# Two chained cross-attention layers on one core: an in-place product with five buffers, first loads and constants inside the first phase, inverses stored once, and new engine orders

## The chip, the cores and the metric

One Trainium2 chip, one of its cores. The time is that of one execution on the device in microseconds (us); the kernel before has a median of 2640.99 us over 3 runs (2639.41 to 2641.47). Engines: PE (TensorE), PEld (its weight loads), DVE (VectorE), ACT (ScalarE), POOL (GpSimd), SP (SyncE, which here issues every DMA).

## The reference

Two cross-attention layers in a row on x (64 batches x 256 tokens x 320 channels), 20 heads of 16, with a context of 77 tokens x 512:

```python
# layer 0
q, k, v = heads(x @ Wq.T), heads(ctx @ Wk.T), heads(ctx @ Wv.T)      # all 77 tokens
x = softmax(q k^T / 4) v @ Wo.T + bo + x
# layer 1: text = ctx[:73], ip = ctx[73:]
q = heads(x @ W_q);  probs_t = softmax(q k_t^T / 4)                  # 73 tokens
text_out = probs_t v_t
qsem = l2norm(probs_t @ text)                                       # per head, 512 wide
sem  = qsem @ l2norm(ip)^T                                          # 4 columns
probs_ip = softmax(q k_ip^T / 4 + 0.5 * sem) * mask                 # 4 columns
out = (text_out + probs_ip v_ip) @ W_out + b_out + x
```

## The kernel before

**First phase** (`keys_and_values`). PE makes keys, values, the Gram matrix of the context tokens and the image-token keys for all batches, in 8 chunks of 8 batches, as sums of three float16 products; ACT and DVE take the results out of PSUM, SP stores them in DRAM (`k_dram`, `v_dram`, `g_dram`, `c_dram`, `kip_dram`). The 616 value rows of a chunk and layer are stored when all five blocks of rows are ready, in two DMAs (L366, L368). A block of the program ends only when all its engines are through, SP's waits for the last stores included.

**Second phase** (`attention`). It begins with clears of tiles (L1161 on DVE, L1281 on POOL), loads of constants (L795) and of the image-token keys (L797, L799). Every engine waits at `all_ready` until all of it is done. Then comes a software pipeline over the 64 batches. In iteration i an engine goes through its string in `ORDER`; a word such as `1u0/3` is step `u`, number 0, of layer 1, for batch i - 3. Every engine works strictly in the order of its string, SP with its DMAs too.

Steps of the PE: `q` query projection, `s` scores (for maxima), `m` transpose of the maxima, `t` turned scores (three products and the maxima subtracted by a product with `sel`), `a` attend (and the sums for the denominators), `o` output projection. Layer 1 only: `u` Gram matrix times halved exponentials, `n` sums of products (the squared norm of the semantic query), `i` image-token scores, `p` attend with the image tokens. Steps `s`, `t` and `a` come in three parts, of which the first two hold two units of four heads and the third one unit.

Other engines: ACT takes q (`q`), maxima (`m`), exponentials (`t0` to `t4`), sums (`a`), makes halves (`h0` to `h4`, tile `eh`), residual plus bias (`r`), the float16 part of what was attended (`g`), norms (`n`), the exponential of the 4 columns (`f`). DVE makes the rest of q (`ql`), maxima (`s0` to `s4`), inverses (`d`), products `w0` to `w4`, the small softmax `y0` to `y20`, `p`, `o`. POOL makes `xh`, `xl` (the float16 parts of the input), `b0` to `b4` (e minus its half, tile `e2`), `at` (attended times inverses), `al`, `kb`, `vb`, `c`.

**The inverses' round trip.** A step `a` leaves denominators in a row of `ust`. SP moves them (`ds`, L837) to `den`; DVE inverts (`d`, L1191); SP stores the inverses in `r_dram` in two copies (`rw`, L861), moves numerators within `ust` (`sh`, four DMAs, L854), and loads the inverses spread over partitions (`rl`, L867) into `rb`. Then POOL `at` (L1297), ACT `g` (L1153), POOL `al` (L1302), PE `o`.

**The product for the norm.** For unit k POOL writes `e2[k % 3]`, DVE writes `wr[k % 3] = psum * e2[k % 3]` (L1198), PE sums `wr` over tokens with `pick` (L1037).

**PSUM.** Eight banks. `USES` lists for each bank the uses in the order of an iteration. A PE step waits until the use before it on each of its banks has been read: a `t` bank by the exponential of its number, an `s` bank by the maxima, an `a` bank by ACT's `a`, a `u` bank by DVE's `w`.

Of the kernel before, what the change touches and what calls it, by code (L numbers as in the profile page):

```python
# [1 line left out]

# [9 lines left out]
ALU = mybir.AluOpType  # L12
# [40 lines left out]
LOW_RING = 3  # L53
# [39 lines left out]
class Batch:  # L93
# [23 lines left out]
    def reached(self, eng, sem, each, k):  # L117
# [21 lines left out]
        1ns/4 1nl/4 1sh/4 1sl/4 1rw/4 1k/2 1st/5 1rl/4 1d/3 1ps/4 1c/2 0x/0 1v/2 1vi/4 1ds/3 1pl/4 0ds/1
        0v/0 0rw/1 0k/0 1ss/3 1g/2 0sh/1 0rl/1""",  # L140
# [82 lines left out]
def keys_and_values(nc, psum, ctx, ctxip, wk, wv, wq, wo, wk_ip, wv_ip, pmask_d, k_dram, v_dram, g_dram, c_dram,  # L223
                    kip_dram, vip_dram, wqs, wos, wqt, wot, rnorm):
# [4 lines left out]
    with ExitStack() as stack:  # L229
# [12 lines left out]
        rawp = [sb(f"raw_projection{n}", [P, CW, WC]) for n in (0, 1)]  # L242
# [41 lines left out]
        s_istored, s_gstored, s_vstored = sem("ip_keys_stored"), sem("gram_stored"), sem("values_stored")  # L284
# [3 lines left out]
        KSTORES, VSTORES = 6, 4  # L288
# [18 lines left out]
        def _(sp):  # L307
# [22 lines left out]
            def store(b, slot):  # L330
# [48 lines left out]
            for n in (0, 1):  # L379
                load_projection(n)  # L380
# [1073 lines left out]
```

## Time and profile before

| | |
|---|---|
| median of 3 runs | 2640.99 us |
| profiled execution, whole | 2627.46 us |
| its span, first to last instruction | 2625.7 us |
| busy share of PE, PEld | 89%, 55% |
| busy share of DVE, ACT, POOL | 66%, 66%, 60% |
| DMA queue q1, share of 16 engines | 41.6% |
| last product of the first phase / first of the second | 333 us / 359.54 us |

A busy share is an average over the first phase (up to 333 us), the filling of the pipeline, about 56 equal iterations and the draining from about 2490 us on. The chain of waits is followed back from the last instruction; a row of it is a stretch of time with what it was spent on. "issue" is time in which the engine waited for nothing that the profile shows; SPq is SP's sequencer issuing a DMA.

### The profile page before, as it was taken

The numbers are of one execution on the slowest core, as the hardware profiler recorded it, in microseconds if no ns is written. First come the engines' busy times: TensorE is split into PE (matmuls) and PEld (weight loads), VectorE is DVE, ScalarE is ACT, GpSimd is POOL, SyncE is SP. The second block draws the span as 40 slices with busy tenths as digits, with TensorE's granted clock in tenths as the row PEclk, the third lists the DMA queues.
The fourth block names the chain that finished last, engine by engine and source line by source line (L and its number), as shares of the span: only waits on it lengthen the run. The fifth ranks groups of instructions, "written<-read, shape, count | busy, mean of one in ns | idle before, by whom it ended". The sixth has DMA issues, their size and how long they took to land.

```text
span 2625.7 us, 90322 instructions
## 1 busy us (share of the span) xinstructions
PE 2329.1 (89%) x35896; PEld 1455.7 (55%) x35896; DVE 1724.0 (66%) x3053; ACT 1728.2 (66%) x2602; POOL 1580.1 (60%) x1055
## 2 busy tenths in 40 slices
PE   7899937989989999998999899999999999899984
PEld 5677724555555555555555555555555555555542
DVE  5533323777777777777777777777777777677764
ACT  3332315777777777777777777777777777777762
POOL 3121024666677666666666667777676666676663
PEclk9999968999999999999999999999999999999996
DMA  8667622343434433334334344334444343434331
GB/s 274 201 211 224 195 82 58 100 110 108 110 102 110 111 106 105 110 108 112 104 109 110 107 109 111 108 107 111 110 112 111 98 112 106 110 106 111 105 90 53
DMA packets 337021, 310.90 MB, mean 118 GB/s; under 512 B 179440, under 2 KB 280048, under 8 KB 336624
## 3 DMA queue, kind: packets, MB, share of 16 engines
q1 hardware_dynamic: 336624, 305.35, 41.6%
q8 instruction: 280, 4.59, 0.7%
q14 instruction: 117, 0.96, 0.1%
HBM read 164.66 MB, written 105.98 MB: 103 GB/s over the span
## 4 chain that ended last, share of the span: by engine, by line
PE 32%; DMA 15%; SPq 14%; ACT 10%; POOL 8%; issue 5%; DVE 3%; ACTq 0%; POOLq 0%; DVEq 0%
PE psum L927 12%; DMA rb<-r_dram 8%; DMA den<-ust 6%; SPq L854 6%; PE psum L1010 5%; ACT ef L1115 5%; PE psum L991 4%; POOL ust L1297 4%; PE psum L1024 4%; POOL al L1302 4%; SPq L861 3%; ACT ah L1153 2%; PE psum L930 2%; SPq L881 1%; ACT ust L1123 1%
## 5 line engine op out<-in xcount | busy, mean ns | idle before, releaser
L1115 ACT ACTIVATE ef<-psum 73x1024 f32<-73x1024 f32 (+1 forms) x640 | 636.9, 1015 | 266.1 <-PE psum L994 248.1
L1335 POOL TENSOR_TENSOR e<-ef,eh 73x1024 f32<-73x1024 f32 x320 | 681.9, 2131 | 81.5 <-ACT eh L1130 81.4
L1176 DVE TENSOR_REDUCE mneg<-psum 128x8 f16<-128x584 f32 (+1 forms) x640 | 464.2, 775 | 105.9 <-PE psum L959 91.5
L1198 DVE TENSOR_TENSOR wr<-psum,e 73x1024 f32<-73x1024 f32 x320 | 390.3, 1220 | 163.6 <-PE psum L1024 160.6
L991 PE MATMUL psum<-q_high,keys 32*73 32x256 f16 (+2 forms) x6144 | 323.8, 258 | 63.1 <-ACT ust L1123 32.0
L1010 PE MATMUL psum<-ef,values 128*32 128x256 f32 x5120 | 357.9, 388 | 4.4 <-DVE wr L1198 4.0
L1024 PE MATMUL psum<-eh,gram 128*73 128x512 f16 x1280 | 338.5, 387 | 12.9 <-ACT ef L1115 11.3
L1297 POOL TENSOR_TENSOR ust<-ust,rb 128x768 f32<-128x768 f32 x128 | 231.7, 1810 | 186.4 <-DMA rb<-r_dram 185.9
L1130 ACT ACTIVATE eh<-ef 73x1024 f16<-73x1024 f32 x320 | 315.6, 1045 | 0.0
L1123 ACT ACTIVATE ust<-psum 128x512 f32<-128x512 f32 x384 | 229.2, 597 | 122.7 <-PE psum L1010 121.9
L991 PEld LDWEIGHTS psum<-q_high,keys 32*73 32x73 f16 (+1 forms) x6144 | 187.6, 110 | 158.4 <-ACT ust L1123 45.5
L1302 POOL TENSOR_TENSOR al<-ust,ah 128x768 f16<-128x768 f32 x128 | 210.4, 1644 | 82.8 <-ACT ah L1153 82.8
L1183 DVE SCALAR_TENSOR_TENSOR q_low<-psum,q_high 128x640 f16<-128x640 f32 x128 | 105.5, 824 | 219.1 <-ACT q_high L1099 219.1
L1327 POOL TENSOR_TENSOR vb<-vi,vmask 96x128 f32<-96x128 f32 x64 | 25.5, 398 | 370.1 <-DMA vi<-vip_dram 370.1
L927 PE MATMUL psum<-ah,wo 128*128 128x256 f16 x1280 | 197.0, 277 | 57.4 <-POOL al L1302 56.9
L1292 POOL TENSOR_TENSOR xl<-x,xh 128x768 f16<-128x768 f32 x128 | 210.4, 1643 | 9.6
L1024 PEld LDWEIGHTS psum<-eh,gram 128*73 128x73 f16 x1280 | 122.2, 114 | 151.9 <-ACT ef L1115 41.2
L994 PE MATMUL psum<-mt,sel 32*73 32x256 f16 (+3 forms) x3072 | 205.4, 251 | 0.8 <-issue 0.8
L991 PE MATMUL psum<-q_low,keys 32*73 32x256 f16 (+3 forms) x3072 | 204.8, 251 | 0.0
L1153 ACT ACTIVATE ah<-ust 128x768 f16<-128x768 f32 x128 | 107.9, 843 | 140.7 <-POOL ust L1297 119.1
L1037 PE MATMUL psum<-wr,pick 128*32 128x256 f32 x2560 | 197.9, 392 | 0.7 <-DVE wr L1198 0.7
L1010 PEld LDWEIGHTS psum<-ef,values 128*32 128x32 f32 x5120 | 128.6, 109 | 118.9 <-issue 41.9
(162 smaller groups left out, 4553.5 us busy)
## 6 DMA issues: line engine op xcount, KB each, us to landing
rb<-r_dram SPq DMA_DIRECT2D x128, 384.0 KB, 4.1
keys<-k_dram SPq DMA_DIRECT2D x128, 231.0 KB, 2.8
values<-v_dram SPq DMA_DIRECT2D x128, 192.5 KB
x<-in_x SPq DMA_DIRECT2D x64, 384.0 KB, 3.6
ust<-ust SPq DMA_DIRECT2D x512, 48.0 KB, 2.1
v_dram<-vst SPq DMA_DIRECT2D x16, 1280.0 KB
out<-outt SPq DMA_DIRECT2D x64, 320.0 KB, 3.2
k_dram<-kst SPq DMA_DIRECT2D x32, 616.0 KB, 4.0
```

Of the source, the lines that this page charges most:

```text
L927: mm = pe.matmul(o[:, c * S:(c + 1) * S], a, data[:, k, :], **at_ends)
L991: pe.matmul(o, keys(l, low, c)[rows, e, 0:n], q[rows, cols], start=(low == 0 and q is qh[l]), stop=False)
L1010: mm = pe.matmul(row(l, f"a{c}")[j * SLOT:(j + 1) * SLOT, r * S:(r + 1) * S], va[l][:, h, :], e, start=True, stop=True)
L1024: mm = pe.matmul(banks(l, f"u{k}", 2)[0:n, r, :], gm[:, half, :], e, start=(half == 0), stop=(half == 1))
L1115: act.activation(ef[l][0:m, unit_heads(n), :].rearrange("t h s -> t (h s)"), src, ACT.Exp, scale=SM).then_inc(s_exp[l], 1)
L1123: act.activation(ust[l][:, b.parity(), :, c, :], src, ACT.Copy).then_inc(s_u[l], 1)
L1130: act.activation(eh[0:m, unit_heads(k), :], ef[1][0:m, unit_heads(k), :], ACT.Copy, scale=0.5)\
L1176: dve.tensor_reduce(dst, o, AX_X, ALU.max, negate=True).then_inc(s_max[l], 1)
L1198: dve.tensor_tensor(wr[0:m, k % LOW_RING, :, :].rearrange("t (r h) s -> t r (h s)", r=2), banks(l, f"u{k}", 2)[0:m, :, :], e2[0:m, k % LOW ...
L1297: pool.tensor_tensor(at(l, b), at(l, b), rb[l][:], ALU.mult).then_inc(s_at[l], 1)
L1302: pool.tensor_tensor(al[l][:], at(l, b), ah[l][:], ALU.subtract).then_inc(s_al[l], 1)
L1335: pool.tensor_tensor(e2[0:m, k % LOW_RING, :, :], ef[1][0:m, unit_heads(k), :], eh[0:m, unit_heads(k), :], ALU.subtract).then_inc(s_e2, 1)
```

## The change

1. **Product in place, five buffers.** `wr` goes. `e2` has five units; DVE multiplies in place; POOL's `b` of a unit waits only for the PE's `n` of the batch before.
2. **Inverses stored once.** `r_dram` has one copy; `rw` is one DMA instead of two, `rl` reads each head's row for 16 partitions instead of 8 + 8.
3. **Beginning of the second phase.** Constants, the first batch's x and (before the last two stores) its layer-0 keys are loaded in the first phase, its `xh` and `xl` made there, `kip` cleared there. `all_ready` goes; single steps wait for the clears. `eh` is cleared by DVE (as the float32 pattern of 128x2560) instead of POOL. Clears that the first steps need (`small_clears`) come first on POOL.
4. **First phase.** Values are stored block by block, five DMAs per chunk and layer, each as its block is ready. `rawp` lies over the raw value weights. The second pair's context is loaded before the output and query projections.
5. **New orders** on all five engines, and new `USES`.

```diff
 ORDER = {
     "pe": """
-        1t1/3 1n3/4 1n4/4 0s0/1 1a0/3 0s1/1 1t2/3 1u0/3 0s2/1 1o/5 0m/1 1u1/3 0o/2 0t0/1 1a1/3 1u2/3 1a2/3
...
+        1t2/3 1a0/3 0s2/1 1o/5 0m/1 1u1/3 0o/2 0t0/1 1u2/3 1a1/3 0t1/1 1q/2 0t2/1 0a0/1 1s0/2 0a1/1 1s1/2
+        0a2/1 1a2/3 1i/2 1s2/2 1u3/3 1m/2 1u4/3 1t0/2 0q/0 1n0/3 1p/4 1n1/3 1n2/3 0s0/0 1n3/3 1n4/3 1t1/2
+        0s1/0 1u0/2""",
...
+        1t3/3 1t4/3 1a0/3 0g/2 1h2/3 0m/1 1h3/3 1r/3 1h4/3 0t0/1 0t1/1 1a1/3 0t2/1 1f/4 0t3/1 1q/2 0t4/1
+        0a0/1 0a1/1 0a2/1 1a2/3 1i/2 1m/2 0r/0 1t0/2 1h0/2 0q/0 1t1/2 1h1/2 1g/4 1n/3 1t2/2""",
...
-        0al/2 1b2/3 1kb/2 1b3/3 1xh/2 1xl/2 1at/4 1vb/4 0xh/0 1b4/3 0xl/0 1c/2 1b0/2 1al/4 1b1/2 0at/1""",
+        1b1/3 1al/5 0at/2 0al/2 1kb/2 1b2/3 1xh/2 1xl/2 1b3/3 1b4/3 0xh/0 0xl/0 1vb/4 1at/4 1c/2 1b0/2""",
...
 USES = [
...
+    "1u1/3 0t1/1 0t3/1 0t4/1 1s0/2 1s3/2 1u3/3 0q/0 0s1/0 0s2/0 1u0/2",
+    "1o/5 0t1/1 0t3/1 0t4/1 1s0/2 1s2/2 1s4/2 1m/2 1t1/2 0s0/0 1t2/2 1u0/2",
...
-                for l in both:
-                    results_of("v", l, 0)
-                    dst = v_dram[l][bass.DynSlice(token, full * P), :].rearrange("(k p) n -> p k n", p=P)
-                    sp.dma_start(dst, vst[l][:, 0:full, :, :].rearrange("p k h d -> p k (h d)")).then_inc(s_vstored, 16)
...
+                    for c, (k0, m) in enumerate(VT):
+                        wait_taken(sp, b, slot, KV_USES.index(("v", l, c, 0)))
+                        dst = v_dram[l][bass.DynSlice(token + k0, m), :]
+                        sp.dma_start(dst, vst[l][0:m, c, :, :].rearrange("p h d -> p (h d)")).then_inc(s_vstored[l], 16)
...
+            for t, d in constants:
+                sp.dma_start(t[:], d).then_inc(s_const, 16)
+            sp.dma_start(early.xin[:], x[0:1, :, :, :].rearrange("a c p s -> p (a c) s")).then_inc(early.s_x, 16)
...
+            sp.wait_ge(s_kstored[0], 16 * KSTORES * 2 * (PAIRS - 1))
+            sp.dma_start(early.ke[:], k_dram[0][0:1, :, :].rearrange("a p n -> (a p) n")).then_inc(early.s_ke, 16)
...
+            pool.wait_ge(early.s_x, 16)
+            pool.tensor_copy(early.xh[:], early.xin[:]).then_inc(early.s_xh, 1)
...
-        dve_clears, pool_clears = [ef[0], ef[1]], [va[0], va[1], eh, wr, kip, mneg[0], mneg[1], gm]
+        small_clears, dve_clears, pool_clears = [mneg[0], mneg[1], va[0], va[1], gm], [ef[0], ef[1], eh], [e2]
...
             def store_inverses(l, b, n):
                 b.reached(sp, s_rd[l], 1, 1)
-                for copy in (0, 1):
-                    dst = r_dram[l][b.parity()][:, copy, :].rearrange("h (q i) -> h q i", i=QS)
-                    sp.dma_start(dst, rd[l][:, b.parity(), :]).then_inc(s_rw[l], 16)
+                dst = r_dram[l][b.parity()].rearrange("h (q i) -> (h q) i", i=QS)
+                sp.dma_start(dst, rd[l][:, b.parity(), :]).then_inc(s_rw[l], 16)
 
             def spread_inverses(l, b, n):
                 b.reached(sp, s_at[l], 1, 0)
-                b.reached(sp, s_rw[l], 32, 32)
-                src = r_dram[l][b.parity()].rearrange("h k n -> (h k) n").unsqueeze(1).to_broadcast([2 * HC, D // 2, CW * S])
+                b.reached(sp, s_rw[l], 16, 16)
+                src = r_dram[l][b.parity()].unsqueeze(1).to_broadcast([HC, D, CW * S])
...
             def weighted(l, b, k):
-                b.reached(dve, f_n, UNITS, k + 1 - LOW_RING if k >= LOW_RING else (4, 5, 3)[k] - UNITS)
                 b.reached(dve, s_e2, UNITS, k + 1)
                 b.reached(dve, f_u, UNITS, k + 1)
                 m = TXT[1]
...
+                rest = e2[0:m, k, :, :].rearrange("t (r h) s -> t r (h s)", r=2)
+                dve.tensor_tensor(rest, banks(l, f"u{k}", 2)[0:m, :, :], rest, ALU.mult).then_inc(s_wr, 1)
```

SP, in the stretch from layer 0's denominators to the spread inverses (`den`, `r_dram`, `ust`, `rb` are those of the round trip above; the suffix of `r_dram` is the batch's parity). Before:

```order
L837 DMA den<-ust 96x1x64
L815 DMA values<-v_dram 77x640
L861 DMA r_dram_1<-rd 8x12x64 x2
L810 DMA keys<-k_dram 128x924
L881 DMA s_dram<-sipst 3x32x256
L820 DMA gram<-g_dram 77x146
L854 DMA ust<-ust 16x768 x4
L867 DMA rb<-r_dram_1 128x1x768
```

After:

```order
L821 DMA values<-v_dram 77x640
L845 DMA den<-ust 96x1x64
L904 DMA pt<-p_dram 96x1x256
L821 DMA values<-v_dram 77x640
L814 DMA keys<-k_dram 128x924
L828 DMA gram<-g_dram 77x146
L868 DMA r_dram_1<-rd 96x64
L845 DMA den<-ust 96x1x64
L874 DMA rb<-r_dram_1 128x1x768
L862 DMA ust<-ust 16x768 x4
```

Between the store of the inverses and their spreading stood keys, image scores, Gram and four moves of numerators; now one move of layer 1's denominators stands there, and the numerators follow the spreading. Layer 1's values (the first row) now come ahead of the denominators' move.

PE, around unit 0 of the Gram product (`eh,gram` 73x512). Rows of 128x2x77 are layer 0's scores `s0`, `s1`; 73x128 are parts of layer 1's `t2`; `ef,values` is `a0`. Before:

```order
L959 MATMUL psum<-keys,q_high 128x2x77 x8
L1010 MATMUL psum<-ef,values 32x256 x8
L959 MATMUL psum<-keys,q_high 128x2x77 x8
L991 MATMUL psum<-q_high,keys 73x128 x4
L991 MATMUL psum<-q_low,keys 73x128 x4
L991 MATMUL psum<-q_high,keys 73x128 x4
L994 MATMUL psum<-mt,sel 73x128 x4
L991 MATMUL psum<-q_high,keys 73x128 x4
L991 MATMUL psum<-q_low,keys 73x128 x4
L991 MATMUL psum<-q_high,keys 73x128 x4
L994 MATMUL psum<-mt,sel 73x128 x4
L1024 MATMUL psum<-eh,gram 73x512 x4
```

After:

```order
L999 MATMUL psum<-mt,sel 73x256 x4
L964 MATMUL psum<-keys,q_high 128x2x77 x8
L1032 MATMUL psum<-eh,gram 73x512 x4
L996 MATMUL psum<-q_high,keys 73x128 x4
L996 MATMUL psum<-q_low,keys 73x128 x4
L996 MATMUL psum<-q_high,keys 73x128 x4
L999 MATMUL psum<-mt,sel 73x128 x4
L996 MATMUL psum<-q_high,keys 73x128 x4
L996 MATMUL psum<-q_low,keys 73x128 x4
L996 MATMUL psum<-q_high,keys 73x128 x4
L999 MATMUL psum<-mt,sel 73x128 x4
L1016 MATMUL psum<-ef,values 32x256 x8
```

Between the end of `t1` (the first row) and `u0` there is now only `s1`; the attend part and `t2` that stood there come behind.

## Rows read from the trace of the kernel before

**Rows 1.** Windows, 600 to 2500: busy us (count) of PE, PEld, DVE, ACT, POOL; PEclk, DMA share.
```profile
600.00:2500.00 1900.00, 1747.52 (x28777) 1055.51 (x28767) 1370.17 (x2408) 1417.37 (x2072) 1310.51 (x896) 1.00 0.40 108
```

**Rows 2.** Timeline of SP (start, us, what): loads of x for batches 6, 62, 63.
```profile
547.77 1.70 SPq L804 DMA_DIRECT2D x<-in_x  x1
...
2450.03 0.40 SPq L804 DMA_DIRECT2D x<-in_x  x1
2484.15 0.40 SPq L804 DMA_DIRECT2D x<-in_x  x1
```

**Rows 3.** Waits of PE, 600 to 2500: us in total, times, longest.
```profile
PE psum L927 <- POOL al L1302: 41.6, 47, 2.4
PE psum L991 <- ACT ust L1123: 26.8, 55, 0.5
PE psum L959 <- issue: 14.0, 54, 0.3
PE psum L959 <- ACT ef L1115: 13.7, 61, 0.5
PE psum L952 <- ACT ef L1115: 11.0, 56, 0.2
PE psum L1024 <- ACT ef L1115: 10.2, 56, 0.2
```

**Rows 4.** Chain that ended last, 1504 to 1525: start, us, what.
```profile
1505.53 3.39 DMA den<-ust
...
1509.59 0.71 SPq L861
...
1514.79 1.21 SPq L854
...
1516.10 3.75 DMA rb<-r_dram
...
1519.98 1.82 POOL ust L1297
...
1521.90 0.85 ACT ah L1153
...
1522.89 1.65 POOL al L1302
```

**Rows 5.** Timelines of ACT, DVE and PE in one iteration: start, us, what.
```profile
1509.02 1.93 ACT L1115 ACTIVATE ef<-psum 73x1024 f32<-73x1024 f32 x2 [1.34 <-PE psum L994]
1516.20 2.91 DVE L1176 TENSOR_REDUCE mneg<-psum 128x8 f16<-128x616 f32 x4 [0.93 <-PE psum L959]
1518.46 1.06 PE L1024 MATMUL psum<-eh,gram 128*73 128x512 f16 x4
```

**Rows 6.** Timelines of SP, DVE, POOL and PE between the phases.
```profile
333.96 0.47 SPq L368 DMA_DIRECT2D v_dram<-vst  x1
340.22 0.38 SPq L795 DMA_DIRECT2D ident<-in_ident  x1
341.36 4.33 DVE L1161 MEMSET ef<- 128x5120 f32 x1 [7.86 <-issue]
341.36 4.37 POOL L1281 MEMSET eh<- 128x5120 f16 x1
346.70 4.33 DVE L1161 MEMSET ef<- 128x5120 f32 x1 [1.01 <-issue]
359.54 1.01 PE L927 MATMUL psum<-xh,wq 128*128 128x256 f16 x4 [26.57 <-POOL xl L1292]
366.37 3.62 DVE L1176 TENSOR_REDUCE mneg<-psum 128x8 f16<-128x616 f32 x5 [0.56 <-PE psum L959]
```

**Rows 7.** DMA issues, 600 to 2500: count, KB each, median us from issue to landing.
```profile
rb<-r_dram SPq DMA_DIRECT2D x112, 384.0 KB, 4.2
ust<-ust SPq DMA_DIRECT2D x448, 48.0 KB, 2.1
```

**Rows 8.** Timeline of PE in the drain.
```profile
2612.99 1.23 PE L1064 MATMUL psum<-pt,vb 32*128 32x256 f32 x6 [12.98 <-DMA pt<-p_dram]
```

More of the change, by code:

```diff
@@ L1 @@
 from contextlib import ExitStack
+from dataclasses import dataclass
 import numpy as np
@@ L241, in keys_and_values @@
             split[name] = sb(f"split_{name}", [P, 2, EC, columns], F16)
[L242 removed]
+        rawp = [raw[v][:].rearrange("p k n -> p (k n)")[:, 0:CW * WC].rearrange("p (k n) -> p k n", n=WC)
+                for v in ("v0", "v1")]
         order = ["k0", "k1", "kt", "ki", "v0", "v1"]
@@ L401, in _ @@
             sp.wait_ge(s_last, 96)
+            sp.wait_ge(s_const, 16 * len(constants))
+            sp.wait_ge(s_keyless, 1)
             for half in (0, 1):
@@ L405, in _ @@
             sp.wait_ge(s_gstored, 16 * 2 * 2 * PAIRS)
-            sp.wait_ge(s_vstored, 16 * VSTORES * 2 * PAIRS)
+            for l in both:
+                sp.wait_ge(s_vstored[l], 16 * VSTORES * 2 * PAIRS)
         @block.tensor
@@ L489, in half_keys, with wait_stored @@
             return ktail[:, half, :, low, e, :]
-        def wait_stored(eng, b, slot, kind, half):
+        def wait_stored(eng, b, slot, kind, half, l):
             if kind in ("k", "kt"):
@@ L518, in chunk @@
                         continue
-                    wait_stored(act, b, slot, kind, half)
+                    wait_stored(act, b, slot, kind, half, l)
                     b.reached(act, s_filled, 2 * KU, slot * KU + u + 1)
@@ L569, in chunk @@
                         continue
-                    wait_stored(dve, b, slot, kind, half)
+                    wait_stored(dve, b, slot, kind, half, l)
                     b.reached(dve, s_filled, 2 * KU, slot * KU + u + 1)
@@ L635, in _ @@
             pool.memset(one[:], 1.0).then_inc(s_one, 1)
+            pool.memset(early.kip[:], 0.0).then_inc(s_keyless, 1)
             for l in both:
@@ L690, in attention @@
         ql = [sb(f"q_low{l}", [P, PW], F16) for l in both]
-        ke = [sb(f"keys{l}", [P, 2 * CW * 2 * T], F16) for l in both]
+        ke = [early.ke, sb("keys1", [P, 2 * CW * 2 * T], F16)]
         va = [sb(f"values{l}", [P, H, SLOT]) for l in both]
@@ L807, in load_keys @@
             def load_keys(l, b, n):
+                if l == 0 and first(b):
+                    return
                 b.reached(sp, f_t[l], CW, 0)
@@ L812, in load_values @@
             def load_values(l, b, n):
+                if first(b):
+                    sp.wait_ge(s_small, SMALL)
                 b.reached(sp, f_a[l], CW, 0)
@@ L817, in load_gram @@
             def load_gram(l, b, n):
+                if first(b):
+                    sp.wait_ge(s_small, SMALL)
                 b.reached(sp, f_u, UNITS, 0)
@@ L1106, in exponentials @@
             def exponentials(l, b, n):
+                if first(b):
+                    act.wait_ge(s_zero, CLEARED)
                 b.reached(act, f_a[l], CW, n // 2 + 1 - CW)
@@ L1167, in maxima @@
                 m = TXT[l]
+                if first(b):
+                    dve.wait_ge(s_small, SMALL)
                 b.reached(dve, f_m[l], 1, 0)
@@ L1279, in _ @@
         def _(pool):
+            for t in small_clears:
+                pool.memset(t[:], 0.0).then_inc(s_small, 1)
             for t in pool_clears:
                 pool.memset(t[:], 0.0).then_inc(s_zero, 1)
-            all_ready(pool)
             def high_input(l, b, n):
+                if l == 0 and first(b):
+                    return
                 b.reached(pool, f_q[l], 1, 0)
@@ L1289, in low_input @@
             def low_input(l, b, n):
+                if l == 0 and first(b):
+                    return
                 b.reached(pool, f_q[l], 1, 0)
@@ L1339, in _ @@
                                    "at": text_attended, "al": low_attended, "c": sem_values, "kb": ip_keys, "vb": ip_values, "b": rests})
+@dataclass
+class Early:
+    ident16: object
+    sel: object
+    pick: object
+    kmask: object
+    vmask: object
+    mask: object
+    bias: list
+    kip: object
+    xin: object
+    xh: object
+    xl: object
+    ke: object
+    s_x: object
+    s_ke: object
+    s_xh: object
+    s_xl: object
 def attention_stack_kernel(nc, x, ctx, ctxip, mask, wq, wk, wv, wo, bias, wk_ip, wv_ip, ident16_d, sel_d, pick_d,
@@ L1354, in attention_stack_kernel @@
     vip_dram = dram("vip_dram", (CW, B * IP, P))
-    r_dram = [[dram(f"r_dram{l}_{n}", (HC, 2, CW * S)) for n in (0, 1)] for l in both]
+    r_dram = [[dram(f"r_dram{l}_{n}", (HC, CW * S)) for n in (0, 1)] for l in both]
     n_dram = dram("n_dram", (P, S))
```

129 lines of the change are left out of this document (60 added, 69 removed), and 14 rows, old and new, of the table USES.

## The prediction

> **What bounds the kernel.** I read the windows first, then the loads of x for the length of an iteration, then PE's waits and the chain. Between 600 and 2500 us PE is busy 1747.5 of 1900 us, 92%, at a granted clock of 1.00, while DVE, ACT and POOL are at 69 to 75% [rows 1]. The loads of x for batches 6 and 62 are 1902.3 us apart, 56 iterations of 33.97 us [rows 2]. So PE works 0.92 x 33.97 = 31.24 us in each and stands 2.73 us. None of its matmuls goes or comes, so 31.24 us is a floor and the new orders can win at most 2.73 us an iteration. PE's waits say what the 2.73 is: 41.6 us for POOL's `al`, 26.8 for ACT's `ust`, and four groups of 10 to 14 us of about 0.2 us each time [rows 3]; over 55.9 iterations that is 0.74, 0.48 and 0.88 us. Some 0.6 is spread over smaller groups. The chain shows why `al` is late: it is the round trip of layer 0's inverses, from 1505.53 to 1524.54 us, of which the two stores, the keys, the scores, the Gram load and four moves of numerators stand between 1509.59 and 1516.10 on SP [rows 4]. This loop closes over PE's order and sets the pace with PE itself.
>
> The rest of the time lies at the ends. The first phase's last store is issued at 333.96, the second phase begins at 340.22, and PE's first product comes at 359.54 [rows 6].
>
> **The iteration, part by part.** I laid the new strings out along PE's 31.24 us with the durations of before. The places that decide:
>
> *The round trip.* `rw` is one DMA, 0.71 us of issue less. Between it and `rl` stands one move. The store must land first. No row has its landing; a 48 KB move within the chip's memory takes 2.1 us, a 384 KB load 4.2 [rows 7]; I take 2.1 (24 KB, near the first) and keep 4.2. So `rl` starts 2.1 us after the inverses instead of 6.5, and the numerators, now behind it, land 3 x 0.6 + 0.6 + 2.1 = 4.5 us after `rl`'s start, against 4.2 for `rb`: they are what is late next. The trip from the denominators' move to `al`'s end is then 3.4 + 0.7 + 2.1 + 4.5 + 1.9 + 1.0 + 1.75 = 15.4 us instead of 19.0 [rows 4]. The move itself stands behind layer 1's values, which now wait for `a2` of layer 1 (0.5 us later). Going by the new strings, 19 us of the iteration lie between layer 0's `a2` and `o`. So the 0.74 us for `al` go. What takes its place on POOL is order: `b1` and layer 1's `al` stand ahead of `at`. `h1` is ready some 4.9 us before the iteration's end; `b1` (2.1), `al` (1.65), `at` (1.8), ACT's `g` and `al` (1.65) end 5 us into the next, and PE comes to `o` at 5.5 us: 0.5 us of slack.
>
> *Unit 0 of the Gram product.* It uses banks 1 and 2 of the new table, behind layer 0's `s2` and layer 1's `t2`. `t1` ends, then only `s1` (0.3 us) lies before `u0`. The exponential `t2` starts 0.1 us after the end of `t1` and takes 1.0 (two in 1.93) [rows 5]; DVE's maxima `s2` come 0.1 us after `s1` and take 0.75 (four in 2.91) [rows 5]. Both end about 1.2 us after `t1`, so PE stands 0.9 us. `u0` takes 1.06, and `t2`, which needs exponential 3, follows it without a wait. This 0.9 replaces the 0.48 us for ACT's `ust`.
>
> *Other places.* `s2` of layer 0 waits for exponential 4 (0.1 to 0.2, as before); `u2` for DVE's `o` (0.1 us, instead of 0.18); `s0` of layer 1 for exponential 4 of layer 0 (0.2, as before); `q` of layer 1 gets `xl` with 0.4 us to spare, and with one product fewer of POOL ahead of it. The product in place has the same operands and shape, 1.22 us: nothing. Five buffers free POOL and DVE of each other; DVE waits at `w` for PE's Gram product, not for buffers, so alone they bring nothing and only allow the new POOL string. Taking a store away frees SP 1.4 us an iteration, which is seen only in the trip above.
>
> The new wait is 0.9 + 0.8 for the short ones + 0.2 left of the scattered 0.6 (the part for late transfers I take as gone) = 1.9 us, an iteration 31.24 + 1.9 = 33.1 us. That is 0.85 less, over 58 iterations (56 and some of the filling): 49 us. The ends of this: all waits as before, 0; all gone but the short ones, 0.8 us in place of 2.73, 112 us.
>
> **The ends of the phases.** The last values' store is now a block of 104 rows after four that are already on their way. The old last stores took from 333.96 to 340.1; a transfer of 2.1 to 4.2 us instead gives 336.5 to 338.5, a gain of 3. In the second phase the first x, its parts, the keys and constants are there, so PE starts at once. But DVE has its clears ahead of the maxima: two of 4.33 us with 1.1 and 1.0 us of pause, as before, and then `eh`. Its 2560 elements cost 2.2 us at the rate of the 5120 in 4.33 [rows 6]; at the full 4.4 of the POOL row it is 2.2 more. So DVE is free at 337 + 1.1 + 4.33 + 1.0 + 4.33 + 0.5 + 2.2 = 350.5, does `ql` (0.8) and begins the maxima at about 351.5 instead of 366.37. Gain up to here 14 us, the 3 included; bounds 10 and 18. PE's first projection is covered by the clears, whatever its clock. Each of the first two round trips, where PE does nothing else, is 2 us shorter (two stores are 1.4, numerators no longer ahead of `rl` 2.5, less the landing): 3 us. In the drain PE stands 13 us for the last small softmax [rows 8], a chain the change leaves as it is; some shorter round trips, 3 us.
>
> On the clear the Trainium skill has a rule (VectorE: DVE Perf Modes, Zero memsets can be issued as uint32): a memset costs one cycle per element whatever the type, and zeros may be written as 4-byte words. By it `eh` is 2560 elements here and the gain stays; the POOL row, 5120 elements of float16 in 4.37 us, agrees with the count by elements, and no row shows a halved one.
>
> In the first phase values' stores are 48 more, of 0.4 us of SP, which waits there for PE's results anyway; PE has no wait on a store in it. The constants add 9 issues before the first results' stores: no reader in the next 20 us. I take 0, bounds -3 and +3.
>
> Sum: 49 + 14 + 3 + 3 = 69 us off the profiled 2627.5: 2558. The median of the runs is 13.5 us above the profiled execution, so 2572 on its scale.
>
> **Rivals.**
> *Ends only.* PE's waits only change their names: the 0.9 us at `u0`, and 0.7 more at `o` because DMAs that land late meet POOL's string with 0.5 us of slack. For it: the gap at `al` varies up to 2.4 us [rows 3]. Against it: the trip is 3.6 us shorter. 2641 - 20 = 2621; with a part of the gain left, 2605 to 2628.
> *Nearly all waits go.* If `t2`'s exponential is earlier than I lay it (DVE and ACT ahead of PE), only the short waits stay: 2641 - 112 - 20 = 2509; half of that way 2535.
> *Slower: layer 1's tail holds layer 0's.* On POOL layer 1's `al` now stands ahead of layer 0's `at`; it needs ACT's `g`, that DVE's `p`, that PE's `p`, that the load of the probabilities, which on SP stands behind the values' wait and the denominators' move. If `al` is more than 0.5 us late, all of it goes into the iteration. The point where it decides is 0.5 + 0.85 + 20/58 = 1.7 us late. At 2.3 us late an iteration is 34.9, and the time 2641 - 20 + 58 x 0.93 = 2675. Against it: by my layout the load lands 3 us before PE's `p`.
> *It doesn't do what it says.* That starting PE earlier moves nothing, since DVE is held by clears: in my sum already; were the clears 8 us longer than laid, 8 us less.
>
> **Numbers.** Forecast 0.62 (own range 2545 to 2600), ends only 0.17, nearly all 0.14, slower 0.05, something within 0.2% of before 0.02. About 0.2%, 5 us, is what a measurement of this kernel tells from no change. Faster 0.93, same 0.02, slower 0.05. The range leaves out the slower case and the outer parts of the two neighbours: 2526 to 2617.
>
> **What would show it.** Right: loads of x 33.1 us apart; PE's wait for `al` gone from the top, a wait of the Gram product (`u0`) for ACT's exponential or DVE's maxima of about 0.9 us in every iteration as its largest; `rl` issued 2 to 2.5 us after the inverses; the first maxima near 351 us; the second phase at 337. Wrong: PE waiting for `al` as long as before (the order on POOL), a wait at `u0` under 0.4 or over 1.5 us, iterations under 32.5 or over 33.8 us, or a first phase that ends other than at 333 us.

## The result, and the profile after

The changed kernel takes 2718.17 us (median of 4 runs, 2710.15 to 2731.16) against 2640.2 of the kernel before beside it: 1.0304 times as long, 95% interval 1.0261 to 1.0347. It is slower, outside the predicted range of 2526 to 2617 us. The profiled execution has a span of 2708.4 us, 82.7 more than before.

Timeline of SP after (start, us, what): loads of x for batches 7 and 63. They answer to [rows 2].

```profile
576.65 0.41 SPq L806 DMA_DIRECT2D x<-in_x  x1
...
2566.55 0.41 SPq L806 DMA_DIRECT2D x<-in_x  x1
```

Before, the load for batch 7 was issued at 583.47 and the last at 2484.15. So the span's 82.7 us split without a rest: up to batch 7 the changed kernel is 6.8 us ahead; the 56 iterations take 1989.9 us instead of 1900.7, 35.53 each instead of 33.94, which is 89.2 more; the draining from the last x to the end takes 141.9 instead of 141.6.

The ends are as forecast. Timelines of SP, DVE, POOL and PE between the phases, after; they answer to [rows 6].

```profile
331.15 1.97 SPq L370 DMA_DIRECT2D v_dram<-vst  x2
336.23 0.65 SPq L797 DMA_DIRECT2D kip<-kip_dram  x1
336.41 0.72 PE L932 MATMUL psum<-xh,wq 128*128 128x256 f16 x4 [4.18 <-PEq L229]
337.36 4.33 DVE L1167 MEMSET ef<- 128x5120 f32 x1 [4.60 <-issue]
...
347.50 2.19 DVE L1167 MEMSET eh<- 128x2560 uint32 x1 [0.48 <-issue]
351.00 1.51 DVE L1183 TENSOR_REDUCE mneg<-psum 128x8 f16<-128x616 f32 x2 [0.63 <-PE psum L964]
```

The second phase starts at 336.2 instead of 340.2, the first maxima at 351.0 instead of 366.37. The loss lies in the iteration. Windows after, 600 to 2500, with the columns of [rows 1]:

```profile
600.00:2500.00 1900.00, 1670.05 (x27534) 1036.07 (x27536) 1306.33 (x2309) 1363.74 (x1983) 1256.32 (x855) 0.98 0.38 102
```

PE has 230 us without work in 1900 instead of 152, and the granted clock is 0.98 instead of 1.00. Waits of PE after, 600 to 2500 (us in total, times, longest), answering to [rows 3]:

```profile
PE psum L932 <- POOL xl L1301: 75.0, 35, 3.7
PE psum L1032 <- DVE mneg L1183: 52.7, 47, 1.4
PE psum L932 <- DVE e L1205: 42.9, 18, 3.1
...
PE psum L932 <- POOL al L1311: 8.2, 13, 1.1
```

The wait for `ust` is gone, the one for `al` nearly, and the forecast one at `u0` is there (second row, 1.1 us each). New are the first and the third. Both stand before layer 0's query projection; together 117.9 us in 53 iterations, 2.2 us each. The third row's releaser is DVE's product in place; I count it with the first, since both rows vanish together in the first experiment. POOL in turn waits for the load of x: waits of POOL, 600 to 2400.

```profile
POOL xh L1294 <- DMA x<-in_x: 330.2, 51, 7.8
```

Before, this wait was 1.0 us in the whole stretch. The chain of the changed kernel shows what makes x late (start, us, what):

```profile
1746.29 0.43 DVE psum L1244
1746.74 0.33 SPq L894
1747.18 0.59 SPq L862
...
1749.70 0.53 SPq L833
1750.33 0.66 SPq L874
1751.09 5.30 DMA x<-in_x
1756.51 0.83 POOL xh L1294
1757.48 1.65 POOL xl L1301
1759.27 1.91 PE psum L932 x16
```

L1244 is `y14` of layer 1, the addition of the visual sums (its tile goes by the name of psum); L894 is `sl`, SP's load of them; L862 numerators, L833 `c`, L874 `rb`, then x. SP stood before `sl` from 1740.91 on, the end of the issue before it. Waits of SP after, 600 to 2500 (L121 is a helper's line; its row here is SP waiting before `rl` for the stored inverses to land):

```profile
SPq L894 <- DVE psum L1244: 304.9, 54, 6.0
SPq L121 <- DMA r_dram<-rd: 156.7, 53, 3.8
```

The first row is 5.6 us in every iteration. The cause can be read in the strings: `sl` was `1sl/4` on SP, DVE's `y` steps are `1y14/4` in both kernels, and `sl` waits for `y14` of the batch before (`SIP_READ - STEPS`). At lag 4 that `y14` had run an iteration earlier. The new string has `1sl/3`, so the `y14` that it waits for is the one of the same iteration. `sip` has two halves, so `y14` two batches back would be enough. And x stands behind it, right behind the 384 KB of `rb`. DMA issues after, 600 to 2500 (count, KB, median us to landing), answering to [rows 7]:

```profile
rb<-r_dram SPq DMA_DIRECT2D x107, 384.0 KB
x<-in_x SPq DMA_DIRECT2D x54, 384.0 KB, 5.8
ust<-ust SPq DMA_DIRECT2D x428, 48.0 KB, 3.0
p_dram<-pip SPq DMA_DIRECT2D x54, 96.0 KB, 4.8
```

Before, x landed in 3.5 us and the store of `p` in 2.0.

Some of the stalls also cost clock. PE's products of layer 0's query projection after a stall of 2.06 us:

```profile
1793.97 0.80 PE L932 MATMUL psum<-xh,wq 128*128 128x256 f16 x4 [2.06 <-POOL xl L1301]
...
1795.42 1.06 PE L932 MATMUL psum<-xh,wq 128*128 128x256 f16 x4
```

The granted clock is 0.50, the level of 1.2 GHz, from 1795 to 1797 and 1.00 again from 1798 on; over 1793 to 1798 it is 0.66. A group of four takes 1.06 us; one iteration earlier, after a stall of 1.40 us, it took 0.60, and the whole projection 2.40 us (from 1759.27) where it takes 4.02 here. So this drop cost 1.6 us beside the stall. Summed over windows of 4 us, 600 to 2400, the clock that was not granted comes to 30.9 us, at most 0.61 an iteration.

### The profile page after: what moved, and what is told of

Same layout as the page of the kernel before. It is cut to its first block, busy times and chain, and to the rows that moved or that the text cites. A ratio compares the mean times of both kernels' runs of the same rounds, so it can differ in the third digit from the quotient of the medians.

```text
span 2708.4 us, 90644 instructions
## 1 busy us (share of the span) xinstructions
PE 2326.6 (86%) x35896; PEld 1487.2 (55%) x35896; DVE 1716.7 (63%) x3054; ACT 1738.2 (64%) x2602; POOL 1583.0 (58%) x1054
## 4 chain that ended last, share of the span: by engine, by line
PE 37%; DMA 17%; SPq 11%; DVE 7%; issue 6%; POOL 5%; ACT 4%; DVEq 0%; POOLq 0%; ACTq 0%
PE psum L932 15%; DMA x<-in_x 6%; SPq L862 6%; PE psum L1032 6%; PE psum L1044 5%; PE psum L996 3%; DMA p_dram<-pip 3%; DMA den<-ust 3%; ACT ef L1121 3%; PE psum L935 3%; DMA ust<-ust 3%; DMA r_dram<-rd 3%; DVE x L1276 2%; PE psum L1016 2%; POOL xl L1301 2%
## 5 line engine op out<-in xcount | busy, mean ns | idle before, releaser
L1183 DVE TENSOR_REDUCE mneg<-psum 128x8 f16<-128x584 f32 (+1 forms) x640 | 471.9, 779 | 120.0 <-PE psum L964 83.3
L1205 DVE TENSOR_TENSOR e<-psum,e 73x1024 f32<-73x1024 f32 x320 | 386.1, 1207 | 81.2 <-PE psum L1032 74.6
L1294 POOL CAST xh<-x 128x768 f16<-128x768 f32 x127 | 104.4, 822 | 499.9 <-DMA x<-in_x 389.1
L1016 PE MATMUL psum<-ef,values 128*32 128x256 f32 x5120 | 346.4, 388 | 7.9 <-DVE pip L1258 5.4
L1136 ACT ACTIVATE eh<-ef 73x1024 f16<-73x1024 f32 x320 | 336.3, 1052 | 16.5 <-ACT ef L1121 0.8
L1129 ACT ACTIVATE ust<-psum 128x512 f32<-128x512 f32 x384 | 222.6, 596 | 110.5 <-PE psum L1016 110.2
L932 PE MATMUL psum<-xh,wq 128*128 128x256 f16 x1024 | 165.9, 288 | 140.2 <-POOL xl L1301 87.5
L996 PEld LDWEIGHTS psum<-q_high,keys 32*73 32x73 f16 (+1 forms) x6144 | 180.0, 110 | 139.4 <-ACT ef L1121 58.6
L932 PE MATMUL psum<-ah,wo 128*128 128x256 f16 x1280 | 195.2, 276 | 22.8 <-POOL al L1311 21.8
L1103 ACT ACTIVATE q_high<-psum 128x640 f16<-128x640 f32 x128 | 90.1, 704 | 168.3 <-PE psum L935 168.3
```

The source lines that it names most:

```text
L932: mm = pe.matmul(o[:, c * S:(c + 1) * S], a, data[:, k, :], **at_ends)
L996: pe.matmul(o, keys(l, low, c)[rows, e, 0:n], q[rows, cols], start=(low == 0 and q is qh[l]), stop=False)
L1016: mm = pe.matmul(row(l, f"a{c}")[j * SLOT:(j + 1) * SLOT, r * S:(r + 1) * S], va[l][:, h, :], e, start=True, stop=True)
L1129: act.activation(ust[l][:, b.parity(), :, c, :], src, ACT.Copy).then_inc(s_u[l], 1)
L1136: act.activation(eh[0:m, unit_heads(k), :], ef[1][0:m, unit_heads(k), :], ACT.Copy, scale=0.5)\
L1183: dve.tensor_reduce(dst, o, AX_X, ALU.max, negate=True).then_inc(s_max[l], 1)
```

## The experiments

Theory: the wait of `sl` holds SP, and what is queued behind it, x above all, is late. Rivals: layer 1's tail on POOL; the bytes ahead of x, not the hold; the product in place or the single store. Ratios are to the kernel before on the same chip; iterations are 56 intervals between x loads unless said. One expectation (32.1 to 32.5 us) rests on a miscount of the loads: the iteration of the first experiment is 32.66 us.

**The wait two batches back.**

```diff
-                b.reached(sp, s_y, STEPS, SIP_READ - STEPS)
+                b.reached(sp, s_y, STEPS, SIP_READ - 2 * STEPS)
```

> The changed kernel, but SP's load of the image scores (sl) waits only for the small softmax of two batches back, whose half of sip it overwrites. Theory A (sl, now a batch ahead of the small softmax, waits for y14 of the batch before in the same iteration and holds numerators, inverses and the next x on SP): the iteration falls from 35.5 to 33.1 to 33.6 us, the time to 2585 to 2620 us, and PE's wait for xl goes. Rival B (POOL's new string alone makes xh and xl late, or the five buffers' waits do): within 10 us of 2718.

Measured: 2532.35 us, ratio 0.9661 (0.9644 to 0.9678); iteration 32.66, shorter than the 33.1 to 33.6 that theory A expected. One number in one wait takes 0.064 off the changed kernel's ratio of 1.0304. Waits of PE, 600 to 2400:

```profile
PE psum L1032 <- DVE mneg L1183: 57.2, 51, 1.4
PE psum L964 <- ACT ef L1121: 15.8, 56, 0.6
...
PE psum L932 <- POOL al L1311: 8.0, 14, 1.9
```

The stall before `q` is gone, POOL's wait for x fell from 330.2 to 43.7 us, though x still lands 5.6 us after its issue. The clock of the stretch is 1.00 again. This confirms the hold, and the rival of POOL's string or the product in place as the cause is out: both are as they were. Against the kernel before the span splits as 21.8 us ahead at batch 7, 71.5 won over 56 iterations, 0.3 in the draining.

**x ahead of the held load**, its wait kept.

```diff
-... 1st/5 1k/2 1sl/3 1sh/4 1c/2 1rl/4 0x/0 1vi/4 ...
+... 1st/5 1k/2 0x/0 1sl/3 1sh/4 1c/2 1rl/4 1vi/4 ...
```

> The changed kernel with the next x's load moved on SP from behind rl of layer 1 to ahead of sl; the wait of sl is as in the changed kernel. Theory A: x is off the loop, PE's wait for xl goes, the iteration is 33.3 to 34 us and the time 2590 to 2630 us; layer 1's numerators and inverses are still held, which is seen but has slack. Rival B: within 10 us of 2718. If this gains much less than the kernel with the shorter wait, the hold costs by another way than x.

Measured: 2583.61 us, 0.9863 (0.9847 to 0.9879), iteration 33.50. x lands in 3.5 us. SP is still held 273.1 us in 53 turns; what is behind it now is the round trip of layer 1, and PE waits 37.6 us for `al`. So two thirds of what the shorter wait wins came through x, and the rest of the hold still costs 0.8 us an iteration.

**x one place earlier**, still behind the hold, ahead of `rl`.

```diff
-... 1sl/3 1sh/4 1c/2 1rl/4 0x/0 1vi/4 ...
+... 1sl/3 1sh/4 1c/2 0x/0 1rl/4 1vi/4 ...
```

> The changed kernel with the next x's load one place earlier on SP: ahead of rl of layer 1, still behind the held sl, numerators and c4. Theory A with the queue as its second half (x lands 5.8 us after issue because the 384 KB of rb are just ahead of it, against 3.6 us before the change): x lands some 2.5 to 3 us earlier, the iteration falls to 33.3 to 34.2 us and the time to 2590 to 2645 us. If only SP's issue order counts and not the bytes ahead, it is 0.7 us earlier: 2680 us.

Measured: 2685.46 us, 1.0249 (1.0232 to 1.0266), iteration 35.26. x lands in 3.5 us and PE's wait for `xl` leaves the list, but the time hardly moves. The gain is 0.0055 of the ratio, 15 us; the 2680 us of the expectation is near only because this chip is faster, and its condition, x landing no earlier, didn't hold. Waits of PE, 600 to 2400:

```profile
PE psum L1070 <- DMA pt<-p_dram: 57.9, 48, 2.2
PE psum L1032 <- DVE mneg L1183: 51.7, 46, 1.4
PE psum L932 <- POOL al L1311: 34.4, 37, 1.9
```

With SP held, other things behind it are late: here `p`, whose store now lands in 5.0 us, and `al`. An order that leaves x behind the hold is no cure.

**The changed kernel with the old strings** (`ORDER` and `USES` of before).

> The changed kernel with ORDER and USES of the kernel before: product in place, five buffers, inverses stored once, early loads and block-wise stores stay. Theory A (the loss is the new strings alone): iteration 33.5 to 34.0 us, time 2600 to 2628 us, some 15 to 20 us of it from the start of the second phase. Rival C (one of the other parts costs per iteration, by the single copy's read pattern or the longer waits of b on PE's n): 2650 us or more.

Measured: 2603.56 us, 0.9944 (0.9927 to 0.9961), iteration 33.78, PE's waits as in [rows 3] (`al` 36.3, `ust` 27.1 in 1800). At batch 7 it is 15.6 us ahead. So the ends, the product in place and the single store are worth 15 us together, and without the new orders there is no loss. That the orders alone make it, this run doesn't show; the last run below takes the single store's part out of it.

**`sl` moved to the end of the string**, wait kept.

```diff
-... 1k/2 1sl/3 1sh/4 ... 1ds/3 0rl/1
+... 1k/2 1sh/4 ... 1ds/3 0rl/1 1sl/3
```

> The changed kernel with one word of SyncE's order moved: layer 1's load of its visual sums (`sl`, with its wait for `y14` of the batch before, unchanged) stands last in the turn instead of ahead of `sh`, `c`, `rl` and the next batch's `x`. If what costs is that this wait holds what is queued behind it, the time is that of the kernel with the shorter wait: 0.965 to 0.975 of the kernel before, x loads 32.1 to 32.5 us apart, x landing 3.5 to 5.8 us after its issue, and no stall of PE for POOL's `xl`. Rival: the load itself comes too late in the turn for layer 1's `i` steps, which it then feeds a turn later: then PE waits for it and the ratio is over 0.99. Second rival: VectorE's `y` steps are late by themselves and everything hung on them stays late: ratio about 1.03.

Measured: 2585.18 us, 0.9829 (0.9808 to 0.985), iteration 33.40. SP no longer waits at `sl` at all, and neither rival's number came; but the gain is only three quarters of the first experiment's. Chain of this kernel:

```profile
1709.56 3.53 DMA r_dram<-rd
1713.15 0.62 SPq L874
1713.87 0.41 SPq L894
...
1716.26 5.43 DMA ust<-ust
1721.76 1.82 POOL ust L1306
```

`sl` now stands between `rl` and layer 0's numerators, which were what is late next in that trip. PE waits 45.5 us for `al`. I take its 96 KB and 0.5 us of issue at this place for the 0.74 us an iteration that are lost against the first experiment; no run moves it again to show it. I had expected it free there.

**The inverses stored twice again**, with the shorter wait.

```diff
-                dst = r_dram[l][b.parity()].rearrange("h (q i) -> (h q) i", i=QS)
-                sp.dma_start(dst, rd[l][:, b.parity(), :]).then_inc(s_rw[l], 16)
+                for copy in (0, 1):
+                    dst = r_dram[l][b.parity()][:, copy, :].rearrange("h (q i) -> h q i", i=QS)
+                    sp.dma_start(dst, rd[l][:, b.parity(), :]).then_inc(s_rw[l], 16)
...
-                src = r_dram[l][b.parity()].unsqueeze(1).to_broadcast([HC, D, CW * S])
+                src = r_dram[l][b.parity()].rearrange("h k n -> (h k) n").unsqueeze(1).to_broadcast([2 * HC, D // 2, CW * S])
```

> The changed kernel with the shorter wait of the visual sums, and with the reciprocals stored twice again (two stores of the same data and a load from both copies, as the kernel before has it). It prices the single store by itself. If the store's count matters as SyncE's issue time only (four more issues of about 0.06 us and their transfers each turn): 0 to 0.3 us each iteration, ratio 0.966 to 0.976. If the load from one copy is slower in DRAM than from two, this kernel is the faster one: `rb` lands earlier than in the kernel with one store, and the ratio is under 0.963.

Measured: 2515.76 us, 0.9558 (0.9542 to 0.9574), iteration 32.41: faster than with one store. PE's wait for `al` is 0.8 us in 1800. DMA issues, 600 to 2400:

```profile
rb<-r_dram SPq DMA_DIRECT2D x111, 384.0 KB, 4.1
x<-in_x SPq DMA_DIRECT2D x55, 384.0 KB, 4.3
n_dram<-nst SPq DMA_DIRECT2D x56, 128.0 KB, 2.4
```

With one store x took 5.6 and `n_dram` 3.5: what is queued behind `rb` lands 1.1 to 1.3 us earlier. The expectation priced the stores too low: a store of 8x12x64 takes SP 0.69 us to issue, twice per layer, where the single one of 96x64 takes 0.40 in the changed kernel. The kernel is faster in spite of it.

**One store, shorter wait, x first**, on the same chip.

> The changed kernel with the shorter wait and with the next x load ahead of `sl`, `sh`, `c` and `rl`. x then lands in about 3.5 us instead of 5.6. If the slack behind x is already enough once the hold is gone, the ratio stays at 0.966 within 0.003. If the late landing still costs, the ratio is 0.955 to 0.963. If x's bytes ahead of the partial sums make `p` late (the load of them took 3.8 us behind an early x, against 2.1), PE waits for `pt` and the ratio is over 0.97.

Measured: 2531.2 us, 0.9612 (0.9596 to 0.9628), iteration 32.79, `al` 12.5 us. The ratio lies in the range that was expected if x's late landing cost, but x at 4.2 us buys nothing that can be told from the first experiment: 0.9661 and 0.965 on other chips, and the kernel with two stores differs as much from chip to chip (0.9558 and 0.9614); the iteration is no shorter either. On this chip it is 15 us behind the kernel with two stores.

**The kernel before without its own hold** (`SEM_READ - 2 * STEPS` at L842).

> The kernel before with its own hold of SyncE taken away: layer 1's store of the denominators waits for `y13` two batches back instead of one. SyncE was held there 82.8 us in 52 turns. If a hold costs only where something behind it has no slack (the theory: 1.6 us here is less than that slack), the ratio is 0.997 to 1.003. If any hold of that queue costs its length, it would be 1.6 us an iteration, ratio about 0.965, the same gain as the changed kernel has without its hold, and the new orders would deserve no credit.

Measured: 2635.3 us, 1.0009 (0.9995 to 1.0023). Its hold of 82.8 us in 52 turns is gone, and SP then waits as much longer at the next line (`ust`, 228.4 instead of 145.8 us). This hold was free, since the next wait ends as late without it. So the 0.966 above is not what any hold's removal gives, but comes from the change, the new orders above all.

**The first experiment again**, as a base.

> The changed kernel with the shorter wait of the visual sums once more, as the base that the next kernels are set against on one chip. Expected from its first run: a ratio of 0.966 to the kernel before, PE waiting 8 us in 1800 for `al`, x landing 5.6 us after its issue. If its place beside the kernel with two stores (0.956) was only the chip's, it comes out at 0.956 here.

Measured: 2531.14 us, 0.965 (0.9622 to 0.9678), iteration 32.63.

**Two stores and x first.**

> The changed kernel with the shorter wait, two stores of the inverses (both copies read) and x ahead of `sl`. If the late landing of x still costs when it is 4.3 us, this is the fastest: 0.950 to 0.954. If x has slack enough, it is 0.956 within 0.002, as with two stores alone.

Measured: 2516.18 us, 0.9593 (0.9564 to 0.9623), iteration 32.42. x has slack enough; on this chip 15 us under the base.

**The kernel before with one store.**

> The kernel before with the inverses stored once and read from one copy, nothing else. The prediction gave the single store a gain: one issue of 0.71 us less on the round trip that the wait for `al` hangs on; with PE's wait for `al` of 0.74 us an iteration that is up to 0.7 x 56 = 39 us, ratio 0.985 to 0.995. Rival: reading one copy takes the queue longer (1.2 to 1.5 us, as x behind it landed 5.6 us in the place of 4.3), and that eats the issue saved or more: ratio 1.000 to 1.015, with `rb` landing at over 5 us or the transfers behind it later.

Measured: 2622.56 us, 1.0021 (0.9997 to 1.0045). PE's wait for `al` rose to 51.9 us in 1800, against 39.2 before. The single store alone gives the kernel before nothing.

**Stored twice, read once.**

```diff
+                src = r_dram[l][b.parity()][:, 0, :].unsqueeze(1).to_broadcast([HC, D, CW * S])
```

> The changed kernel with the shorter wait, the inverses stored twice, but the spreading load reading only the first copy (128 partitions, 16 of them the same row, in place of 8 and 8). It tells the number of stores apart from the source of the load. If the source is what costs, x lands at 5.5 us and PE waits for `al` as in the kernel with one store: 0.966, or a little slower for the second store's issue. If the store is what costs (one store of 24 KB landing late), it is 0.956 as with two stores read twice, with x at 4.3 us.

Measured: 2537.36 us, 0.9675 (0.9648 to 0.9703), x at 5.6 us. No faster than with one store, and 6 us slower than the base of this chip (2531.14): the load's source is what costs. The 6 us may be the second store; no run shows it apart. Two things differ in that source: one copy or two, and 8 rows read 16 times or 16 rows read 8 times. The next two take them apart.

**One copy, a pattern of 16 rows**, and **two copies, a pattern of 8 rows**.

The first with one store, the second with two:

```diff
+                src = bass.AP(tensor=r_dram[l][b.parity()].tensor, offset=0, ap=[[256, 2 * HC], [0, D // 2], [1, CW * S]])
...
+                src = bass.AP(tensor=r_dram[l][b.parity()].tensor, offset=0, ap=[[2 * CW * S, HC], [CW * S // D, D], [1, CW * S]])
```

Both leave out that each inverse reaches its own element, so they compute something else; the 384 KB that the load writes are the same.

> The changed kernel with the shorter wait and one store of the inverses; the spreading load takes as many bytes from the same single copy, but its source pattern is 16 rows (each 256 elements behind the one before, so they overlap) read 8 times each, in place of 8 rows read 16 times. Which inverse reaches which partition is changed by that; the work is the same. If the row count of the pattern is what costs, x behind the load lands at 4.3 us as with two copies, PE hardly waits for `al`, and the ratio is 0.954 to 0.960. If the single copy in DRAM is what costs, it is as with one store: x at 5.6 us, PE's wait for `al` 8 us in 1800, 0.964 to 0.968. The Trainium skill (DMA: Bandwidth & Descriptors, Why a DMA increments its semaphore by 16 and not by 1) says that a DMA is split over the largest number of engines up to 16 that divides the slowest dimension of both its patterns; by that rule 8 rows would put the load on 8 of 16 engines, and this kernel would be the fast one.

> The changed kernel with the shorter wait and the inverses stored twice; the spreading load reads from both copies, but with a source pattern of 8 rows (16 reads for each, at steps of 48 elements through the head's two copies). Which inverse reaches which element is changed by that; the bytes are the same. If the row count costs, this one is slow: x lands at 5.5 us, no landing of `rb` can be paired with its issue, and the ratio is 0.964 to 0.970. If reading one copy costs, it is fast, 0.954 to 0.960.

Measured: 16 rows from one copy 2515.25 us, 0.9614 (0.9594 to 0.9633), iteration 32.41; 8 rows from two copies 2539.52 us, 0.9713 (0.9692 to 0.9734), iteration 32.74. DMA issues, 600 to 2400, of the first:

```profile
rb<-r_dram SPq DMA_DIRECT2D x111, 384.0 KB, 4.0
x<-in_x SPq DMA_DIRECT2D x55, 384.0 KB, 4.3
```

and of the second:

```profile
rb<-r_dram SPq DMA_DIRECT2D x110, 384.0 KB
x<-in_x SPq DMA_DIRECT2D x55, 384.0 KB, 5.6
```

Both ratios lie just above their expected ranges, but so does that of the kernel with two stores on this chip (0.9614 in the next run, 0.9558 and 0.9593 elsewhere); between the two it is 24 us. The count of rows decides, the copies don't. The share of the 16 DMA engines that is busy while `rb` moves shows how: one microsecond, from 1.5 to 2.5 us after an issue of `rb`, in the kernel with 16 rows and in the one with 8, with the columns of [rows 1] (the last but one is the share).

```profile
1727.47:1728.47 1.00, 1.00 (x35) 0.78 (x24) 0.93 (x4) 0.61 (x2) 1.00 (x2) 1.00 0.92 313
1707.57:1708.57 1.00, 1.00 (x11) 0.90 (x10) 0.43 (x1) 1.00 (x2) 1.00 (x1) 1.00 0.47 169
```

Over all 55 such issues of layer 1 between 600 and 2400 the median share is 0.93 and 0.45. The Trainium skill (DMA: Bandwidth & Descriptors, Why a DMA increments its semaphore by 16 and not by 1) says that a DMA goes to the largest number of engines, up to 16, that divides the slowest dimension of both its patterns, and that only those engines count its completion. By it 8 rows would keep half the engines out. The runs agree in both directions, and the shares of 0.93 and 0.45 fit 16 engines and 8; which engines carry the load no row here shows. The landing, too, is in the trace for `rb` with 16 rows and not with 8, and for the store of the inverses as 96x64 and not as 8x12x64.

**Two stores, shorter wait, again.**

> The changed kernel with the shorter wait and two stores, once more, as the base on this chip: 0.956 to 0.960, x landing 4.3 us after its issue.

Measured: 2515.81 us, 0.9614 (0.9595 to 0.9634). The same as one store with 16 rows, so with 16 rows the second store itself costs nothing that can be measured. With 8 rows on this chip the loss is 24 us.

**The hold kept, two stores.**

> The changed kernel with its own wait kept (SyncE held by `sl`) and the inverses stored twice, both read. If hold and slow load add up, it is 0.006 to 0.010 faster than the changed kernel: a ratio of 1.020 to 1.025. If x's landing is on the path that the hold sets, the 1.3 us that x lands earlier counts in full each iteration: 56 x 1.3 = 73 us, ratio 1.003. If the second store's issue lies on the held stretch too, 0.7 us more: 1.02.

Measured: 2598.51 us, 0.9935 (0.9912 to 0.9957), iteration 33.78. SP is held as in the changed kernel. Waits, 600 to 2400, of PE, SP and POOL:

```profile
PE psum L933 <- POOL xl L1302: 57.7, 51, 2.9
...
SPq L895 <- DVE psum L1245: 274.8, 53, 5.7
...
POOL xh L1295 <- DMA x<-in_x: 288.6, 54, 7.0
```

x lands in 4.5 us instead of 5.8, the store of `p` in 3.6 instead of 4.8. So the load's 8 rows cost 15 to 24 us where nothing is held, and 3.7% (some 97 us) behind the hold, more than I had expected of any case: 1.75 us an iteration. PE's stall before layer 0's `q` is 1.1 us an iteration shorter (1.1 here, 2.2 there), x's landing 1.3 us. The clock not granted, summed in windows of 4 us from 600 to 2400, is 8.5 us here and 30.9 there, 0.16 and 0.61 an iteration, so up to 0.45 us of the difference is clock. The last 0.2 us stay open.

With 16 rows the hold still costs 83 us (2598.51 against 2515.81), with 8 rows 0.064 of the ratio, some 170. Neither the hold nor the 8 rows makes the kernel slower than the one before by itself: the loss needs both.

| | one store, 8 rows | two stores, 16 rows |
|---|---|---|
| `sl` waits for the batch before | 1.0304 | 0.9935 |
| `sl` waits for two batches back | 0.9661, 0.965 | 0.9558, 0.9614 |

## Why the prediction was wrong

*The ends* were right: second phase at 336.2 (337 forecast), maxima at 351.0 (351.5), `eh` cleared in 2.19 us (2.2). The kernel with the old strings shows 15 us for them. *The drain* gave 0.3 us instead of 3.

*Unit 0* was right: 1.1 us each, forecast 0.9, and the largest wait of PE in all kernels with the new orders and without the hold.

*The wait of `sl`* is the step that failed; it was put at nothing. Of what the new order of SP makes wait, the prediction has one thing: "The move itself stands behind layer 1's values, which now wait for `a2` of layer 1". I went through what stands on SP between the inverses and `rl` of layer 0, and never asked of the other words with a new lag what they wait for. `sl` went from lag 4 to 3 with a wait written for lag 4. It holds SP 5.6 us, and PE then stands 2.2 us before layer 0's `q` for the x behind it. "Other places" has layer 1's `xl` with 0.4 us to spare; layer 0's, which hangs on the load of x, was never in the sum. That step turned the sign: with the wait two batches back the same kernel is 0.966, or 2551 us on the scale of 2641, within the own range of 2545 to 2600.

*The single store* was counted as a gain of 0.71 us of issue ("Taking a store away frees SP 1.4 us an iteration"), with the landing of `rb` taken from [rows 7] as 4.2. The load had changed its pattern, so that row didn't hold for it. What is queued behind it lands 1.3 us later. Alone that is 15 us, which the forecast would have borne; behind the hold it is 97, and without it the sign would not have turned either (0.9935).

*The round trip's* other terms were too short. `rl` was to be issued 2 to 2.5 us after the inverses; it comes 4.1 us after the issue of their store (median, layer 0, 600 to 2400), 3.7 in the first experiment and 6.1 before. A move of numerators lands in 3.0 us, not 2.1. The wait for `al` fell to 8 us all the same.

*The floor* of 31.24 us of PE's work was too high. In the first experiment PE is busy 1685 of 1800 us (600 to 2400), 30.6 us an iteration, with 2.1 idle where 1.9 was forecast. The matmuls are the same; I take it that their modelled times overlap more in one order than in another, but no run shows that apart. The iteration came out 0.4 under the 33.1 forecast for that.

*The rivals.* The slower one had the right kind of mechanism, something queued behind a waiting instruction, at the wrong engine: PE's wait for layer 0's `al` on POOL fell from 41.6 to 8.2 us. It had 0.05, and that its side came true is luck. No rival named the wait of `sl`. The list of what would show the prediction wrong did catch it: iterations over 33.8 us.

## What to carry to other kernels

Where a step changes its lag, work out again for each wait in it which iteration the awaited event falls in; on a queue that issues in order, price the wait by what stands behind it, not by what it waits for. Give such a wait the full depth of its buffer. And when a DMA's access pattern changes, its duration before is no longer a row for it: a source of 8 rows instead of 16 made what stands right behind a 384 KB load land 1.1 to 1.3 us late. Two losses that are small or bearable by themselves can multiply on one queue: test them together.

## What the runs showed of the hardware

- The same 384 KB load holds back what is queued behind it 1.1 to 1.3 us longer with 8 source rows than with 16 (x 5.6 and 4.3 us, `n_dram` 3.5 and 2.4), while the busy share of the DMA engines as it moves is 0.45 instead of 0.93. In the kernel before, with its old orders, the same switch moved `n_dram` by 0.5 us only (3.4 to 3.9) and x, which isn't right behind `rb` there, hardly (3.5 and 3.4).
- A small transfer lands late behind a burst: the store of `p`, 96 KB, took 1.8 to 2.8 us to land in the kernels in which SP isn't held before `sl`, and 3.6 to 5.0 in those in which it is and then issues the delayed transfers at once.
- PE stood 53 times before layer 0's `q` in the changed kernel, 600 to 2500. After 19 of these stalls, of 2.01 to 3.66 us, the granted clock of the 5 us from the first product on was 0.66 to 0.73, that is 1.2 GHz for some three of them; after 16 others of 2.04 to 3.07 us, and after all 18 shorter ones, it was 1.00. So a longer stall brought the drop only about half the time.
- SP's holds come with very different prices: 1.6 us an iteration for nothing (1.0009), 5.2 us for 3% with a load of 16 rows behind it, 5.6 us for 6% with one of 8.
- The best kernels here are the changed one with the wait two batches back and a spreading load of 16 rows: 0.956 to 0.961 of the kernel before.
